# Routed expert blocks: hidden transposes and down products one block later, last additions split anew, one choice ahead of a copy

## The chip, the cores and the metric

One core of a Trainium2 chip runs the whole program in one launch. The metric is the device time of an execution in microseconds, median over the runs. TensorE (PE) multiplies matrices into PSUM, VectorE (DVE), ScalarE (ACT) and GpSimd (POOL) work on vectors, and SyncE (SP) issues most of the DMAs. Each engine works through its own list of instructions in order, and engines wait for each other on semaphores.

## The reference, cut to what matters

Eight sequences of 128 tokens with 128 features go through gated cross-attention with 16 heads and then through a mixture of experts:

```python
x = x + tanh(g_xattn[0]) * attention(layernorm(x), ctx, ctx, mask, Wq, Wk, Wv, Wo, 16)
h = layernorm(x)                                    # 1024 tokens x 128
shared = (silu(h @ shared_gate.T) * (h @ shared_up.T)) @ shared_down.T
probs = sigmoid(h @ router_w.T + routing_bias)      # 8 experts
scores, indices = top_k(probs, 2); scores = scores / sum(scores)
g = silu(einsum('th,ehi->tei', h, gate_w)); u = einsum('th,ehi->tei', h, up_w)
combined = einsum('tei,eih,te->th', g * u, down_w, w)   # w: scores at the two chosen experts
x = x + tanh(g_ffn[0]) * (shared + combined)
```

The hidden width of each expert is 256. All is in float32.

## The kernel before

**Attention and routing.** The attention runs over pairs of batches. As soon as a batch is through, its second layernorm, its logits, the choice of two experts for each token and the place of each token in its expert's list are worked out, in five groups: batches 0 and 1, 2 and 3, 4 and 5, then 6, then 7. `choose_steps(r)` (L1002) makes the choice of group r on VectorE in five steps, the last of which writes `hot`; `ranks(r)` (L451) counts on TensorE; `place(r)` (L1045) turns the ranks into slots; `scatter(r)` (L1356) on GpSimd writes the rows of the chosen tokens to the DRAM table `xs` with indirect DMAs. GpSimd's list after the attention is: scatters of group 2 (batches 4 and 5) with the two reciprocal deviations of batches 6 and 7 between them, the counts of groups 2 and 3, the scatters of batches 6 and 7 (L1431 to L1438). On VectorE the choice of group 2 stands around the copy `copy_pt(14, 2)` (L955, L1214 to L1220), which moves transposed probabilities from PSUM to SBUF for TensorE.

**Routed blocks.** The rows in `xs` are sorted by expert and cut into 23 blocks (`BLOCKS`) of 128 slots; how many of them hold rows depends on the data. `EARLY` is 5: so many blocks are fetched before batches 6 and 7 are placed. For each block n:

- SyncE fetches its rows from `xs` into buffer n modulo 8 of `xg` (`gather`, L290). From block 8 on it first waits until the result of block n-8 has been written, since that write reads its row numbers from the same buffer.
- TensorE transposes the rows (`block_transpose`, L631; "gather transpose"), ScalarE and VectorE split them into a high and a low part (L848, L1243), and TensorE makes gate and up products in three passes (`block_gate_up`, L640).
- ScalarE applies SiLU (L854), VectorE multiplies (`block_hidden`, L1248) to `hid`.
- TensorE transposes `hid` (`block_hidden_transpose`, L648; "hidden transposes", two, into the one bank `hT_bank`), VectorE copies the result to SBUF (`block_hidT`, L1254), and TensorE makes the down product (`block_down`, L657).
- ScalarE scales it by the token's weight into `y_sb` (`block_y`, L860), and GpSimd writes it with an indirect DMA to the DRAM table `ys` (L1441).

The order is written out by hand: iteration n of TensorE's loop (L673) issues the gather transpose of block n+2, gate and up of block n+1, the down product of block n-1 and the hidden transposes of block n. ScalarE and VectorE have loops of the same kind (L869, L1269). Products of the shared expert (`shared_pass`, `down_step`) are put in at iteration 3 and after the loop.

**The end.** When the last block with rows is written (SyncE's waits at L314), SyncE loads `ys` in four parts of two batches (`load_y`, L221). GpSimd adds the first chosen expert's rows to `x_sb` (L1447), then VectorE adds the second's (L1292), and for each half VectorE adds the shared expert's product from PSUM (`add_shared`, L1205). `store_out` (L225) stores two batches at a time, two on SyncE's queue and two on ScalarE's.

Of the kernel before, what the change touches and what calls it, by code (L numbers as in the profile page):

```python
# [6 lines left out]
ALU = mybir.AluOpType  # L7
# [28 lines left out]
LAST = len(ROUTED) - 1  # L36
SEEN = 6
EARLY = (SEEN * P * TOP_K - E_ROUTED * (P - 1)) // P + 1
PAD_ROWS = SLOTS // P // 5
IN_FLIGHT = 8  # L40
FEWEST = TOKENS * TOP_K // P // IN_FLIGHT
# [14 lines left out]
def build(nc, x, ctxT, mask, wqT, wkT, wvT, woT, gu, down, routerT, rows, ident, before, out):  # L56
    with ExitStack() as stack:
# [6 lines left out]
        def sem(name):  # L64
            return stack.enter_context(nc.semaphore(name))
# [19 lines left out]
        x_sb = sb("x_sb", [P, B, P])  # L85
# [124 lines left out]
        tx_done, xghi_ready, xglo_ready = sem("tx_done"), sem("xghi_ready"), sem("xglo_ready")  # L210
        bg_done, sil_ready, hid_ready = sem("bg_done"), sem("sil_ready"), sem("hid_ready")
        th_done, hidT_ready, yb_done, y_ready = sem("th_done"), sem("hidT_ready"), sem("yb_done"), sem("y_ready")
        first_added, second_added = sem("first_added"), sem("second_added")

        xs = nc.dram_tensor("xs", (SLOTS, WIDTH), F32).ap()
        ys = nc.dram_tensor("ys", (TOP_K * TOKENS, P), F32).ap()
# [7 lines left out]

        def store_out(engine, n):  # L225
            tiles = slice(2 * n, 2 * n + 2)
            engine.wait_ge(acc_done, 1 + n // 2)
            engine.dma_start(out[:, tiles, :], x_sb[:, tiles, :]).then_inc(out_sem, 16)

        block = stack.enter_context(nc.Block())  # L230
# [94 lines left out]
        def _(pe):  # L325
# [322 lines left out]
            def block_hidden_transpose(n):  # L648

                pe.wait_ge(hid_ready, n + 1)  # L650
                if n:
                    pe.wait_ge(hidT_ready, n)
                for c in range(2):
                    mm = pe.transpose(hT_bank[:, c * P:(c + 1) * P], hid[n % 2][:, c * P:(c + 1) * P], ident_sb[:])
                mm.then_inc(th_done, 1)
# [17 lines left out]
            for n in range(BLOCKS):  # L673
                if n + 2 == EARLY:
                    pe.wait_ge(h_done, 1)
                    shared_pass(1, 0)
                    shared_pass(1, 1)
                if n + 2 < BLOCKS:
                    block_transpose(n + 2)
                if n + 1 < BLOCKS:  # L680
                    block_gate_up(n + 1, experts[n + 1])
                if n + 2 < BLOCKS:
                    experts[n + 2] = block_expert(n + 2)
                if n:
                    block_down(n - 1, experts.pop(n - 1))
                block_hidden_transpose(n)
            pe.wait_ge(xglo_ready, BLOCKS)
            shared_pass(2, 0)
            block_down(BLOCKS - 1, experts[BLOCKS - 1])
            shared_pass(2, 1)  # L690
            pe.wait_ge(hid_ready, BLOCKS)
            shared_pass(3, 0)
            shared_pass(3, 1)
            down_step(0)
# [4 lines left out]
        def _(act):  # L699
# [169 lines left out]
            for n in range(BLOCKS):  # L869
                if n + 2 < BLOCKS:  # L870
                    block_hi(n + 2)
                if n + 1 < BLOCKS:
                    block_silu(n + 1)
                if n:
                    block_y(n - 1)
                if n == 0:
                    silu(0)
                if n + 2 == EARLY:
                    silu(1)
            block_y(BLOCKS - 1)  # L880
            for unit in range(2, 4):
                silu(unit)
# [5 lines left out]
        def _(dve):  # L888
# [215 lines left out]
            def run(steps, count):  # L1104
                for _ in range(count):
                    next(steps, None)

            def finish(steps):
                for _ in steps:
                    pass  # L1110
# [102 lines left out]
            mask_max(15, PAIRS - 1, 3, chain(after(2, x2_lo, 2), after(5, copy_o, 13, 1)))  # L1213
            recips(15, 3, (0,))  # L1214
            choice = choose_steps(2)
            run(choice, 1)
            copy_pt(14, 2)
            run(choice, 1)
            recips(15, 3, (1,))
            finish(choice)  # L1220
            finish(weight_steps(2))
            place(2)
            add_attention(B - 2, use)
# [43 lines left out]
            run(last_table, 3)  # L1267
            block_hidden(0)
            for n in range(BLOCKS):  # L1269
                if n:  # L1270
                    block_hidT(n - 1)
                run(last_table, 1)
                if n + 2 < BLOCKS:
                    block_lo(n + 2)
                if n == 1:
                    hidden(0)
                run(last_table, 1)
                if n + 1 < BLOCKS:
                    block_hidden(n + 1)
                run(last_table, 1)  # L1280
                if n + 1 == EARLY:
                    hidden(1)
                if n == 2 * EARLY:
                    quota_steps()
            block_hidT(BLOCKS - 1)
            for unit in range(2, 4):
                hidden(unit)
            for half in range(2):
                for n in (2 * half, 2 * half + 1):
                    tiles = slice(2 * n, 2 * n + 2)  # L1290
                    dve.wait_ge(first_added, n + 1)
                    dve.tensor_tensor(x_sb[:, tiles, :], y_of[:, tiles, 1, :], x_sb[:, tiles, :], ALU.add).then_inc(second_added, 1)  # L1292
                dve.wait_ge(second_added, 2 * half + 2)
                add_shared(half)


        @block.gpsimd
        def _(pool):
# [140 lines left out]
            for n in range(BLOCKS):  # L1439
# [1 line left out]
                pool.indirect_dma_start(out=ys, out_offset=bass.IndirectOffsetOnAxis(  # L1441
                    ap=xg[n % IN_FLIGHT][:, P:P + 1].bitcast(U32), axis=0), in_=y_sb[n % IN_FLIGHT][:], in_offset=None,
                    bounds_check=TOP_K * TOKENS - 1, oob_is_err=False).then_inc(y_out[n % IN_FLIGHT], 16)
            for n in range(4):
                tiles = slice(2 * n, 2 * n + 2)
                pool.wait_ge(in_y[n], 16)
                pool.tensor_tensor(x_sb[:, tiles, :], y_of[:, tiles, 0, :], x_sb[:, tiles, :], ALU.add).then_inc(first_added, 1)  # L1447


# [37 lines left out]
```

## Time and profile before

| what | value |
|---|---|
| median of 3 runs | 179.69 us (179.23 to 180.6) |
| the profiled execution | 180.42 us, its span 178.4 us |
| busy share of the span | PE 92%, DVE 71%, ACT 61%, POOL 62% |
| chain that ended last | PE 50%, DVE 13%, ACT 9%, DMA 9%, POOL 9%, issue 6% |
| granted TensorE clock | full until TensorE's work is over, half in the last slice |
| routed blocks | first gather transpose 123.74, last down product 165.36 |
| TensorE's last product ends | 171.7 us |

Times in the rows are microseconds from the start of the span. A busy TensorE is one with instructions in flight, not one at its peak. PE rows are matmuls (a transpose is one too), PEld rows their weight loads. The span is the time from the first to the last instruction of the profiled execution.

### The profile page before, as it was taken

How to read it: one execution, taken by the hardware profiler on the slowest of the kernel's cores; microseconds unless marked ns; L12 is line 12 of the kernel's file. 1: busy time of each engine (PE TensorE's matmuls, PEld its weight loads, DVE VectorE, ACT ScalarE, POOL GpSimd, SP SyncE). 2: the span in 40 equal slices, each digit the busy share in tenths (PEclk: the TensorE clock that was granted, in tenths of full speed). 3: DMA queues.
4: the chain of work that ended last, by engine and by line, in shares of the span. 5: the costliest groups of instructions: out<-in, count | busy, mean ns of one | idle time of the engine just before them, and what ended most of it. 6: DMA issues, size and time to landing. Idle time of an engine off the chain costs nothing.

```text
span 178.4 us, 4673 instructions
## 1 busy us (share of the span) xinstructions
PE 164.0 (92%) x1412; PEld 139.4 (78%) x1412; DVE 127.0 (71%) x611; ACT 109.3 (61%) x403; POOL 111.4 (62%) x141
## 2 busy tenths in 40 slices
PE   7899889999999999999999999988999999998950
PEld 7687669997879998879998778976586878786840
DVE  2789988755898776788676878877947666664344
ACT  4566997558697457787547878535446656564300
POOL 3665799846786825867714858686544665666460
PEclk9999999999999999999999999999999999999995
DMA  5899995810000000000000000013222322221253
GB/s 164 252 371 371 416 397 215 338 73 0 18 2 5 13 2 4 30 21 21 24 4 0 15 21 17 15 49 86 66 77 65 72 61 72 66 64 42 53 189 118
DMA packets 11095, 17.34 MB, mean 97 GB/s; under 512 B 2075, under 2 KB 6945, under 8 KB 10944
## 3 DMA queue, kind: packets, MB, share of 16 engines
q1 hardware_dynamic: 9504, 14.59, 24.3%
q0 software_dynamic: 1280, 2.20, 3.7%
q8 instruction: 12, 0.20, 0.5%
q10 hardware_dynamic: 288, 0.26, 0.4%
q14 instruction: 11, 0.09, 0.2%
HBM read 9.99 MB, written 7.51 MB: 98 GB/s over the span
## 4 chain that ended last, share of the span: by engine, by line
PE 50%; DVE 13%; ACT 9%; DMA 9%; POOL 9%; issue 6%; SPq 1%; POOLq 0%
PE misc L408 8%; PE s_even L371 6%; PE o_bank L397 6%; ACT probs L727 4%; PE pt L382 4%; DMA ys<-probsT,xg 3%; PE pt L663 3%; PE proj_q L328 3%; DMA wq_raw<-wqT 3%; PE proj_k L328 3%; DVE probs L939 3%; POOL ys L1441 2%; PE proj_k L330 2%; PE proj_k L329 2%; PE proj_q L330 2%
## 5 line engine op out<-in xcount | busy, mean ns | idle before, releaser
L727 ACT ACTIVATE probs<-probs,negmax 128x128 f32<-128x128 f32 x128 | 50.0, 395 | 8.5 <-DVE negmax L939 8.5
L1332 POOL TENSOR_TENSOR probs<-probs,rinv 128x512 f32<-128x512 f32 x32 | 33.1, 1046 | 24.6 <-DVE rinv L953 24.4
L1441 POOL DMA_INDIRECT ys<-probsT,xg x23 | 22.5, 979 | 17.3 <-issue 10.2
L727 ACT ACTIVATION_READ_ACCUMULATOR probs<-probs,negmax 128x1 f32 x128 | 24.5, 191 | 0.0
L939 DVE CUSTOM_DVE_ANT_0 probs<-s_even,mask 128x128 f32<-128x128 f32 x64 | 18.1, 283 | 3.8 <-issue 3.8
L1362 POOL DMA_INDIRECT xs<-xrow,slot x16 | 16.2, 1011 | 6.8 <-issue 3.9
L382 PE MATMUL pt<-ident_sb,probs 128*128 128x128 f32 x128 | 17.6, 277 | 1.6 <-POOL probs L1332 1.1
L371 PE MATMUL s_odd<-kT,qT 64*128 64x128 f32 x128 | 18.5, 285 | 0.0
L371 PE MATMUL s_even<-kT,qT 64*128 64x128 f32 x128 | 18.5, 285 | 0.0
L939 DVE CUSTOM_DVE_ANT_0 probs<-s_odd,mask 128x128 f32<-128x128 f32 x64 | 18.2, 284 | 0.0
L663 PEld LDWEIGHTS pt<-down_sb,v 128*128 128x128 f32 x92 | 12.1, 190 | 7.6 <-issue 7.5
L716 ACT COPY qT<-proj_q 128x512 f32<-128x512 f32 x12 | 7.1, 588 | 16.8 <-PE proj_q L330 16.8
L371 PEld LDWEIGHTS s_even<-kT,qT 64*128 64x128 f32 x128 | 15.4, 187 | 2.1 <-issue 1.4
L663 PE MATMUL pt<-down_sb,v 128*128 x92 | 15.7, 293 | 1.5 <-DVE v L1258 1.5
L382 PEld LDWEIGHTS pt<-ident_sb,probs 128*128 128x128 f32 x128 | 14.1, 141 | 3.4 <-issue 1.8
L397 PE MATMUL o_bank<-probsT,v 128*64 128x128 f32 x240 | 16.4, 279 | 0.0
L397 PEld LDWEIGHTS o_bank<-probsT,v 128*64 128x64 f32 x240 | 12.8, 136 | 3.4 <-issue 2.5
L371 PEld LDWEIGHTS s_odd<-kT,qT 64*128 64x128 f32 x128 | 15.4, 187 | 0.0
L408 PE MATMUL misc<-wo_sb,oT 128*128 128x128 f32 x112 | 14.3, 281 | 1.0 <-DVE oT L961 1.0
L408 PEld LDWEIGHTS misc<-wo_sb,oT 128*128 128x128 f32 x112 | 13.0, 192 | 2.0 <-DVE oT L961 1.7
L864 ACT ACTIVATE probsT<-pt,xg 128x128 f32<-128x128 f32 x23 | 8.5, 368 | 6.6 <-PE pt L663 4.9
L926 DVE COPY kT<-proj_k 128x512 f32<-128x512 f32 x12 | 8.3, 692 | 5.8 <-PE proj_k L330 5.6
(287 smaller groups left out, 457.2 us busy)
## 6 DMA issues: line engine op xcount, KB each, us to landing
xs<-pad SPq DMA_DIRECT2D x5, 858.0 KB, 5.6
xg<-xs SPq DMA_DIRECT2D x23, 66.0 KB, 1.9
down_sb<-down SPq DMA_DIRECT2D x1, 1152.0 KB, 9.0
probs<-ys SPq DMA_DIRECT2D x4, 256.0 KB, 4.1
gu_raw<-gu SPq DMA_DIRECT2D x3, 256.0 KB, 6.4
wk_raw<-wkT SPq DMA_DIRECT2D x2, 256.0 KB, 4.0
wq_raw<-wqT SPq DMA_DIRECT2D x2, 256.0 KB, 5.4
mask<-mask SPq DMA_DIRECT2D x8, 64.0 KB, 2.0
```

The costliest lines, as they stand in the source:

```text
L328: pe.matmul(dst, a_hi, b_hi, start=True, stop=False)
L371: mm = pe.matmul(s_bank[odd][:, j * P:(j + 1) * P], qT[rows, 4 * half + j, i * P:(i + 1) * P], kT[rows, 4 * half + j, i * P:(i + 1) * P], ...
L382: mm = pe.transpose(pt_bank[u][:, j * P:(j + 1) * P], probs[:, r, 4 * u + j, :], ident_sb[:])
L397: mm = pe.matmul(o_of.get(g, o_bank)[DK * odd:DK * (odd + 1), j * P:(j + 1) * P], v_sb[i][:, h * DK:(h + 1) * DK], probsT[:, half, 2 * j + ...
L408: mm = pe.matmul(misc[:, 0:P], oT[:, c // 4, c % 4, :], wo_sb[:, c, :], start=(c == 0), stop=(c == CHUNKS - 1))
L663: mm = pe.matmul(y_bank[:, 0:P], hidT[n % 2][:, c, :], down_sb[:, bass.ds(e * I_FFN + c * P, P)], start=(c == 0), stop=(c == 1))
L727: e = act.activation(probs[:, r, l, :], probs[:, r, l, :], ACT.Exp, bias=negmax[:, r, l:l + 1], scale=-1.0, accum_out=rowsum[:, r, l:l + 1])
L864: act.activation(y_sb[n % IN_FLIGHT][:], y_bank[:, 0:P], ACT.Copy, scale=xg[n % IN_FLIGHT][:, P + 1:P + 2]).then_inc(y_ready, 1)
L939: dve.tensor_tensor_reduce(probs[:, r, l, :], s_bank[l % 2][:, (l // 2) * P:(l // 2 + 1) * P], mask_sb[r // 2][:], -1.0, HUGE, ALU.add, AL ...
L1332: pool.tensor_tensor(quad, quad, rinv[:, r, 4 * u:4 * u + 4].unsqueeze(2).to_broadcast([P, 4, P]), ALU.mult).then_inc(norm_done, 1)
L1362: pool.indirect_dma_start(out=xs, out_offset=bass.IndirectOffsetOnAxis(ap=slot[:, b, k:k + 1], axis=0), in_=xrow[:, b, k, :], in_offset=No ...
L1441: pool.indirect_dma_start(out=ys, out_offset=bass.IndirectOffsetOnAxis(ap=xg[n % IN_FLIGHT][:, P:P + 1].bitcast(U32), axis=0), in_=y_sb[n ...
```

## The change

It has three parts. In the routed loop, from block 3 on (`FIRST` is 3), TensorE issues the hidden transposes of block n-1 in iteration n, right behind gate and up of block n+1, and then the down product of block n-2, where it had issued the down product of n-1 and the hidden transposes of n. ScalarE's and VectorE's lists follow. After the loop the last hidden transposes and the two last down products stand between the shared products. In the routing of batches 4 and 5 VectorE's copy `copy_pt(14, 2)` goes from the second step of the choice to behind it. At the end VectorE adds both experts' rows for the first four batches after the shared part; for the last four GpSimd adds the two experts' rows to each other and VectorE adds the sum. A store now waits for the additions of its own two batches.

```diff
...
 LAST = len(ROUTED) - 1
 SEEN = 6
 EARLY = (SEEN * P * TOP_K - E_ROUTED * (P - 1)) // P + 1
+FIRST = EARLY - 2
 PAD_ROWS = SLOTS // P // 5
 IN_FLIGHT = 8
 FEWEST = TOKENS * TOP_K // P // IN_FLIGHT
...
-        first_added, second_added = sem("first_added"), sem("second_added")
+        rows_added, pair_added = sem("rows_added"), sem("pair_added")
 
         xs = nc.dram_tensor("xs", (SLOTS, WIDTH), F32).ap()
         ys = nc.dram_tensor("ys", (TOP_K * TOKENS, P), F32).ap()
...
 
         def store_out(engine, n):
             tiles = slice(2 * n, 2 * n + 2)
-            engine.wait_ge(acc_done, 1 + n // 2)
+            engine.wait_ge(rows_added, (2, 4, 5, 6)[n])
             engine.dma_start(out[:, tiles, :], x_sb[:, tiles, :]).then_inc(out_sem, 16)
 
         block = stack.enter_context(nc.Block())
...
                     block_gate_up(n + 1, experts[n + 1])
                 if n + 2 < BLOCKS:
                     experts[n + 2] = block_expert(n + 2)
-                if n:
+                if n > FIRST:
+                    block_hidden_transpose(n - 1)
+                if 1 <= n <= FIRST:
                     block_down(n - 1, experts.pop(n - 1))
-                block_hidden_transpose(n)
+                if n < FIRST:
+                    block_hidden_transpose(n)
+                if n > FIRST + 1:
+                    block_down(n - 2, experts.pop(n - 2))
             pe.wait_ge(xglo_ready, BLOCKS)
             shared_pass(2, 0)
-            block_down(BLOCKS - 1, experts[BLOCKS - 1])
+            block_hidden_transpose(BLOCKS - 1)
+            block_down(BLOCKS - 2, experts.pop(BLOCKS - 2))
             shared_pass(2, 1)
-            pe.wait_ge(hid_ready, BLOCKS)
+            block_down(BLOCKS - 1, experts.pop(BLOCKS - 1))
             shared_pass(3, 0)
             shared_pass(3, 1)
             down_step(0)
...
                     block_hi(n + 2)
                 if n + 1 < BLOCKS:
                     block_silu(n + 1)
-                if n:
+                if 1 <= n <= FIRST:
                     block_y(n - 1)
+                if n > FIRST + 1:
+                    block_y(n - 2)
                 if n == 0:
                     silu(0)
                 if n + 2 == EARLY:
                     silu(1)
+            block_y(BLOCKS - 2)
             block_y(BLOCKS - 1)
             for unit in range(2, 4):
                 silu(unit)
...
             mask_max(15, PAIRS - 1, 3, chain(after(2, x2_lo, 2), after(5, copy_o, 13, 1)))
             recips(15, 3, (0,))
             choice = choose_steps(2)
-            run(choice, 1)
-            copy_pt(14, 2)
-            run(choice, 1)
+            run(choice, 2)
             recips(15, 3, (1,))
             finish(choice)
+            copy_pt(14, 2)
             finish(weight_steps(2))
             place(2)
             add_attention(B - 2, use)
...
             run(last_table, 3)
             block_hidden(0)
             for n in range(BLOCKS):
-                if n:
+                if 1 <= n <= FIRST:
                     block_hidT(n - 1)
                 run(last_table, 1)
                 if n + 2 < BLOCKS:
...
                 if n == 1:
                     hidden(0)
                 run(last_table, 1)
+                if n > FIRST:
+                    block_hidT(n - 1)
                 if n + 1 < BLOCKS:
                     block_hidden(n + 1)
                 run(last_table, 1)
...
             block_hidT(BLOCKS - 1)
             for unit in range(2, 4):
                 hidden(unit)
-            for half in range(2):
-                for n in (2 * half, 2 * half + 1):
-                    tiles = slice(2 * n, 2 * n + 2)
-                    dve.wait_ge(first_added, n + 1)
-                    dve.tensor_tensor(x_sb[:, tiles, :], y_of[:, tiles, 1, :], x_sb[:, tiles, :], ALU.add).then_inc(second_added, 1)
-                dve.wait_ge(second_added, 2 * half + 2)
-                add_shared(half)
+            def add_rows(n, k):
+                tiles = slice(2 * n, 2 * n + 2)
+                dve.wait_ge(in_y[n], 16)
+                dve.tensor_tensor(x_sb[:, tiles, :], y_of[:, tiles, k, :], x_sb[:, tiles, :], ALU.add).then_inc(rows_added, 1)
+
+            add_shared(0)
+            for n in range(2):
+                dve.wait_ge(acc_done, 1)
+                add_rows(n, 0)
+                dve.wait_ge(rows_added, 2 * n + 1)
+                add_rows(n, 1)
+            add_shared(1)
+            dve.wait_ge(acc_done, 2)
+            for n in range(2, 4):
+                dve.wait_ge(pair_added, n - 1)
+                add_rows(n, 0)
 
 
         @block.gpsimd
...
                 pool.indirect_dma_start(out=ys, out_offset=bass.IndirectOffsetOnAxis(
                     ap=xg[n % IN_FLIGHT][:, P:P + 1].bitcast(U32), axis=0), in_=y_sb[n % IN_FLIGHT][:], in_offset=None,
                     bounds_check=TOP_K * TOKENS - 1, oob_is_err=False).then_inc(y_out[n % IN_FLIGHT], 16)
-            for n in range(4):
+            for n in range(2, 4):
                 tiles = slice(2 * n, 2 * n + 2)
                 pool.wait_ge(in_y[n], 16)
-                pool.tensor_tensor(x_sb[:, tiles, :], y_of[:, tiles, 0, :], x_sb[:, tiles, :], ALU.add).then_inc(first_added, 1)
+                pool.tensor_tensor(y_of[:, tiles, 0, :], y_of[:, tiles, 0, :], y_of[:, tiles, 1, :], ALU.add).then_inc(pair_added, 1)
 
 
 def kernel(x, ctx_1024, fside_Bx1xSxS2_0, g_xattn, g_ffn, L0_xattn_Wq, L0_xattn_Wk, L0_xattn_Wv, L0_xattn_Wo,
```

## Rows read from the trace of the kernel before

**Rows 1.** Timeline, 148 to 152, one loop iteration: start, duration, engine, line, operation, operands.
```profile
148.71 0.27 PE L638 MATMUL misc<-ident_sb,xg 128*128 128x128 f32 x1
...
149.53 0.69 PE L663 MATMUL pt<-down_sb,v 128*128 x4
...
150.06 0.38 PE L654 MATMUL pt<-ident_sb,kT 128*128 128x128 f32 x2
...
150.26 0.37 ACT L864 ACTIVATE probsT<-pt,xg 128x128 f32<-128x128 f32 x1 [0.15 <-PE pt L663]
...
150.48 0.42 DVE L1258 COPY v<-pt 128x256 f32<-128x256 f32 x1
...
151.09 0.66 PE L663 MATMUL pt<-down_sb,v 128*128 x4
...
151.40 0.98 POOL L1441 DMA_INDIRECT ys<-probsT,xg  x1 [0.58 <-issue]
```

**Rows 2.** The chain of waits, 148 to 154: start, duration, what.
```profile
148.31 3.27 DMA ys<-probsT,xg
...
151.74 1.82 DMA xg<-xs
...
153.61 0.33 PE o_bank L638
```

**Rows 3.** One line, L1441 (block writes), 140 to 160.
```profile
DMA to landing us min/median/max: 2.2/2.3/3.3
```

**Rows 4.** One line, L293 (block fetches), 138 to 158: who waited (us, times), and landing.
```profile
  PEld o_bank L638: 0.3, 1
...
DMA to landing us min/median/max: 1.8/2.0/2.7
```

**Rows 5.** Timeline, TensorE, a down product that waits.
```profile
136.70 0.71 PE L663 MATMUL pt<-down_sb,v 128*128 x4 [0.34 <-DVE v L1258]
```

**Rows 6.** Timeline: low part of block 6; gather transposes of blocks 10 and 22.
```profile
134.81 0.29 DVE L1245 TENSOR_TENSOR xg_lo<-o_bank,xg_hi 128x128 fp32r<-128x128 f32 x1 [0.31 <-ACT xg_hi L852]
...
140.55 0.27 PE L638 MATMUL o_bank<-ident_sb,xg 128*128 128x128 f32 x1
...
159.98 0.27 PE L638 MATMUL o_bank<-ident_sb,xg 128*128 128x128 f32 x1
```

**Rows 7.** The chain of waits, 164 to 171.
```profile
164.19 2.76 DMA ys<-probsT,xg
...
167.23 3.70 DMA probs<-ys
```

**Rows 8.** Timeline, block 20's down product, and the last additions.
```profile
162.30 0.71 PE L663 MATMUL pt<-down_sb,v 128*128 x4
...
171.00 3.13 POOL L1447 TENSOR_TENSOR x_sb<-probs,x_sb 128x256 f32<-128x256 f32 x4 [2.78 <-DMA probs<-ys]
171.76 1.79 DVE L1292 TENSOR_TENSOR x_sb<-probs,x_sb 128x256 f32<-128x256 f32 x2 [2.26 <-POOL x_sb L1447]
...
174.26 0.75 DVE L1292 TENSOR_TENSOR x_sb<-probs,x_sb 128x256 f32<-128x256 f32 x2
...
175.04 0.75 DVE L1209 SCALAR_TENSOR_TENSOR x_sb<-proj_q,tanh_g,x_sb 128x512 f32<-128x512 f32 x1
```

**Rows 9.** Timeline, 111 to 115, the choice for batches 4 and 5.
```profile
111.42 2.10 POOL L1332 TENSOR_TENSOR probs<-probs,rinv 128x512 f32<-128x512 f32 x2
111.52 0.69 DVE L957 COPY probsT<-pt 128x512 f32<-128x512 f32 x1
...
113.08 0.49 DVE L1026 TENSOR_TENSOR hot<-rows_sb,chosen_at 128x32 bf16<-128x32 f32 x1
...
113.67 0.17 PE L463 MATMUL proj_q<-hotsum,ones_bf 128*128 128x8 bf16 x1
...
114.88 1.01 POOL L1362 DMA_INDIRECT xs<-xrow,slot  x1 [1.36 <-DVE slot L1053]
```

**Rows 10.** The chain of waits, GpSimd's count of batch 6.
```profile
121.44 0.21 POOL hotsum L1354
```

## The prediction

> **What bounds it now.** I read the busy times by engine first, then the chain of waits, then the timeline of the routed blocks. TensorE is busy for 92% of the span (the table above), so the loop over 23 blocks looks like TensorE's. One iteration shows how: gather transpose at 148.71, down product at 149.53, hidden transposes at 150.06, the next down product at 151.09 [rows 1]: 1.56 us an iteration, 1.53 in the neighbouring one, mean 1.545. Inside it the hidden transposes at 150.06 feed a VectorE copy at 150.48 to 150.90, and the down product at 151.09 uses that copy: the gather transpose and the gate-up product fill just this gap. So the loop has two nearly equal limits, and this is the one the change relaxes.
>
> A third limit is outside the engines. Block n's result lets block n+8's rows be fetched, because both use one of eight buffers. The chain shows that turn once: the indirect write of block 10 starts at 148.31 and takes 3.27, the fetch of block 18 starts at 151.74 and takes 1.82, and TensorE begins block 18's transpose at 153.61, having waited [rows 2]. The median write takes 2.3 and the median fetch 2.0 [rows 3, 4]; only that one gather transpose of the whole stretch had to wait [rows 4]. What matters is how much room the other turns had.
>
> **The turn, worked out.** From the end of ScalarE's copy of y (150.26+0.37 = 150.63) to the start of GpSimd's write (151.40) is 0.77 [rows 1]. The chain has 0.16 from the landing of the write to the fetch (151.58 to 151.74) and 0.05 from the fetch's landing to the transpose [rows 2]. With medians: 0.77+2.3+0.16+1.95+0.05 = 5.2 us. The down product starts 0.82 into its iteration (149.53-148.71) and y is finished 1.10 after it (150.63-149.53) [rows 1].
>
> Before: block n's down product runs in iteration n+1, block n+8's gather transpose opens iteration n+6. The turn needs 0.82+1.10+5.2 = 7.1 us and has five iterations, 7.7: 0.6 to spare at the median, nothing with a 3.27 write, as seen.
>
> After: from block 3 on the down product runs in iteration n+2, behind hidden transposes of 0.22, thus at 1.04. The turn needs 1.04+1.10+5.2 = 7.35 and has four iterations, 6.2. **It does not fit.** Each turn waits 1.15 us, and the loop's pace becomes 7.35/4 = 1.84 us an iteration wherever such turns follow on each other.
>
> **Parts of the change.** (a) *The loop up to the last fetch.* Removed: waits of TensorE on VectorE's hidden copy, of which the one ahead of the down product at 136.70 is shown (0.34 idle, 0.5 with the drained pipeline) [rows 5]; there are two more, 0.28 near 146.4 and 0.60 near 163.8. Ahead of the first stands a limit that stays: block 6's low part, at 134.81 for 0.29 [rows 6], comes behind a wide SiLU on ScalarE, and block 6's gate-up cannot precede 135.15. Then come 0.71 of it, 0.22 transposes, 0.5 down product, which puts block 8's gather transpose at 136.6 to 136.75, and two iterations later block 10's at about 139.85, 0.7 earlier than its 140.55 [rows 6]. From there the turns are 10 to 14 to 18 to 22 in gather transposes four blocks apart, three turns: 139.85+3x7.35 = 161.9, against 159.98 now [rows 6]: +1.95. The other ladders (11, 15, 19) give within 0.3 of it. (b) *The order at the end.* SyncE's last wait is for the write of block 20, at 164.19 for 2.76, and then the loads of y, 3.70 to the first [rows 7]: the blocks after 20 don't set the end. Block 20's down product is now at 162.30 [rows 8], 2.32 after block 22's gather transpose. In the new order come 0.11 gather, 0.71 gate-up 21, 0.22, 0.50, 0.71 gate-up 22, 0.22 transposes of block 20 at +2.25; the transposes of block 21 follow one down product later, but share one PSUM bank and wait for the copy, 1.03 behind as in [rows 1] (150.06 to 151.09): +3.28; then 0.22, and the down product at +3.50. That is +1.2. Sum of (a) and (b) +3.15; one long write such as the 3.27 that already cost a wait will lie on a turn in most executions, for which I add 0.15: **+3.3**. Bounds: all transfers at their minima (2.2 and 1.8) give +2.1; writes and fetches as long as in this execution block by block, its 3.27 write and 2.7 fetch among them, give +4.0.
>
> The later order on ScalarE and VectorE costs nothing by itself: the y copy stands behind the same SiLU, the hidden copy ahead of the hidden product delays that by 0.3, and its reader is the gate-up product two iterations on. If that cover went, at most 0.3 per block would show. GpSimd's 23 writes are the same and come less often than now. SyncE issues the same 23 fetches in order; each now waits behind its later write, which is the turn above.
>
> (c) *The choice ahead of the copy.* The 0.69 copy at 111.52 goes behind the choice. The choice's last operation, hot, starts at 113.08 and takes 0.49 for 32 elements a partition; GpSimd's normalising, two instructions in 2.10 from 111.42, ends just then, at 113.52 [rows 9]. VectorE must wait for the exponentials until 112.13 anyway, so hot starts only 0.1 earlier, and I take it to end no sooner. And the ranks on TensorE start at 113.67, right behind four transposes: TensorE's own order holds them. So the gain is 0 (bound: -0.1). The copy then lies between hot and the weights and slots: GpSimd's scatter at 114.88, which had waited 1.36 for the slots [rows 9], comes 0.64 later. From it GpSimd runs through to the count of batch 6 at 121.44 [rows 10], in the chain of waits all the way, and TensorE's ranks and the first fetch behind it are late next. **+0.6**; bounds 0 (a cover I did not see) and +0.7.
>
> The Trainium skill, "SBUF — State Buffer", section "Who interferes with whom", says that a VectorE instruction with two SBUF inputs and a GpSimd instruction that reads SBUF block each other wholly, whoever issues first. The row of hot agrees. Without that rule hot would keep its 0.49 and end 0.1 sooner, and (c) would be 0.1 less.
>
> (d) *The last additions.* Now, after the first load lands at 170.93: four GpSimd additions from 171.00, 3.13 together; two VectorE additions beside them, 1.79 together; a shared part of 0.75; two additions undisturbed, 0.75 together; and the last shared part at 175.04, 0.75 [rows 8], so the last store goes at 4.86 behind the load. New: the first shared part is done before. The loads land at most 0.8 apart (GpSimd's four additions follow on each other). VectorE: four additions of 0.38 with 0.05 between, to +1.7; shared part to +2.5; GpSimd adds pairs from +1.6 and +2.4 to +3.2; VectorE's fifth addition, disturbed, 0.9, to +3.4; the sixth to +3.8. 4.86-3.8 = **-1.1**. Bounds: -1.4 undisturbed, -0.5 if every VectorE addition costs 0.9. The second shared part needs TensorE's last product. That ends 9.4 after block 20's down product now (171.7, the table) and no more than that in the new order: 165.6+0.6+9.4 = 175.6 at the latest, wanted at 174.8+1.7 = 176.5: covered by 0.9. The first one's products end 1.9 sooner, 173.7, and its 0.75 fits ahead of the load at 174.8.
>
> By the same rule of "SBUF — State Buffer", the pair additions and VectorE's would exclude each other: the fifth then ends at about +3.5 and the sixth at +3.9, 0.1 more than the sum has.
>
> **Sum.** 3.3+0.6-1.1 = +2.8 us on this execution's 180.42 (span 178.4 and 2.0 around it): 183.2. The median of the runs is 179.69, 0.73 lower, so **182.5**.
>
> **Rivals.** *1. The turn is hidden (not slower).* Place: the gather transposes of blocks 11 to 22. If the transit were under 4.05 instead of 5.2, the turn would fit four iterations; then the removed waits (about 0.9) nearly pay for (b), +0.3 in all, and with (d) and (c) the change gives -0.8 to -0.2, 179.2 at the middle. For it: before, all but one turn were covered. Against: the minima already sum to 0.77+2.2+0.16+1.8 = 4.9 [rows 1 to 4]. But rows of one execution could mislead me on which write frees which fetch, and TensorE's order could be looser. 0.20; of this 0.08, with (c) at 0 and (d) at -1.4, gives more than 1% faster. *2. Only the choice is free:* TensorE or the loads hide it; 182.5-0.6 = 181.9. For it: nothing in the chain; chance 0.12. *3. Turns as long as the worst seen:* +4.0, with (d) at -0.5: +4.1, 183.8. For it the 3.27 write; against it that more waiting means fewer transfers at once. 0.16. *4. The change in the tail fails* because the second shared part waits for TensorE: TensorE's work would have to stretch by 0.9. 0.02, near 183.5.
>
> **Numbers.** My forecast has 0.50 (181.5 to 183.4), the rivals 0.20, 0.12, 0.16, 0.02. About 1% (1.8 us) is what a measurement here can tell from none: bounds 177.9 and 181.5. Slower by more: 0.44 of the forecast, 0.08 of rival 2, rivals 3 and 4 whole: 0.70. Within: the other 0.06 and 0.04, and 0.12 of rival 1: 0.22. Faster: 0.08. The range leaves out the faster part of rival 1 and the far end of rival 3: 179.3 to 184.1. Where the turn decides (0.80) its own range is 180.9 to 184.1.
>
> **What would show it.** Waits of TensorE's weight load for the fetch, ahead of the gather transposes of blocks 11, 15, 17 to 19 and 21, together 2.5 to 4.5 us, where there was one of 0.3. No waits ahead of down products in the loop, save the last two blocks. The scatter behind the slots near 115.5 and the first fetch 0.6 later. From the first load of y to the last store 3.8. I am wrong if the gather transposes come 1.55 apart throughout, or if ranks for batches 4 and 5 start before 113.5.

## The result, and the profile after

| | before | after |
|---|---|---|
| median of 4 runs each | 180.11 us (179.23 to 180.6) | 184.42 us (184.35 to 185.16) |
| ratio | | 1.0241 [1.0201, 1.028] |
| the profiled execution, its span | 180.42, 178.4 | 185.16, 183.2 |

The change makes the kernel 4.3 us slower. The forecast was slower by 2.8, with 182.5 and a range that ends at 184.1: the direction and the mechanism hold, the size does not.

The two spans differ by 4.8. Cut at events that both traces have, that is:

| stretch | before | after | difference | forecast |
|---|---|---|---|---|
| start to the exponentials of batches 4 and 5 | 110.81 | 111.52 | +0.7 | none |
| from there to the first gather transpose | 12.93 | 13.58 | +0.65 | +0.6 |
| from there to block 20's write landed | 43.21 | 47.64 | +4.4 | +3.3 |
| to the first load of y landed | 3.98 | 3.82 | -0.2 | none |
| to VectorE's last addition | 4.86 | 3.65 | -1.2 | -1.1 |
| to the end of the span | 2.59 | 2.97 | +0.4 | none |

The exponentials are ScalarE's for the logits of batches 4 and 5, 110.81 and 111.52. The first line is no part of the change: it arises in the first 12 us, when weights are loaded (ScalarE's first copy of weights starts at 3.98 before and at 4.61 after). Without it the stretches add up to 4.1, where the medians differ by 4.3.

**The turn.** The line of the gather transposes after, with what its engines waited for (the columns are us, times; TensorE's matmuls and its weight loads are counted apart, so 12 is six blocks):

```profile
  DMA xg<-xs: 9.5, 12
```

Before, one block waited 0.3 [rows 4]. Now six do, blocks 11, 15, 17, 18, 21 and 22, and the weight load alone waits 5.3 of the 9.5. The chain of waits after (start, us, what) has three times a write, a fetch and the gather transpose that waits for it:

```profile
139.41 2.31 DMA ys<-probsT,xg
...
141.88 1.91 DMA xg<-xs
143.84 0.33 PE misc L639
144.17 0.37 PE s_even L329
...
146.85 0.77 POOL ys L1461
...
148.33 0.76 POOL ys L1461
...
149.80 0.78 POOL ys L1461
...
151.29 3.71 DMA ys<-probsT,xg
...
155.16 2.00 DMA xg<-xs
157.21 0.33 PE o_bank L639
...
160.21 2.37 DMA ys<-probsT,xg
...
162.74 2.10 DMA xg<-xs
164.89 0.33 PE o_bank L639
```

Block 3's write brings block 11, block 10's brings block 18, and block 14's brings block 22. Between them the chain runs along GpSimd's writes of blocks 7 to 10, which start 1.48 apart, the pace of TensorE's iterations there; block 10's starts 0.77 behind ScalarE's copy of y as well, as the prediction has it. 143.84 is block 11 and the transpose of block 15 comes at 151.20, 7.36 later, the turn worked out in the prediction as 7.35. The transpose of block 14 is at 148.46, though, and that of block 18 at 157.21, 8.75 later, because the write of block 10 takes 3.71, where [rows 2] had 3.27. Block 22 comes another 7.68 later. Of the chain from 139.4 to the landing of block 20's write, half is now writes and fetches (16.5 of 33.3 us); over the whole span the page has DMA at 13% of the chain, where it had 9%, and TensorE at 46%, where it had 50%:

```profile
PE 46%; DMA 13%; DVE 11%; ACT 10%; POOL 8%; issue 8%; SPq 1%; DVEq 0%; POOLq 0%; ACTq 0%
```

**The order at the end.** Block 20's down product, in the timeline of TensorE:

```profile
164.89 0.33 PE L639 MATMUL o_bank<-ident_sb,xg 128*128 128x128 f32 x1 [0.65 <-DMA xg<-xs]
...
168.24 0.41 PE L655 MATMUL pt<-ident_sb,kT 128*128 128x128 f32 x2 [0.16 <-DVE v L1267]
168.73 0.37 PE L664 MATMUL pt<-down_sb,v 128*128 x1
```

That is 3.84 behind block 22's gather transpose, where it was 2.32 [rows 6, 8]: +1.5, with +1.2 forecast.

**The choice**, in the timeline (start, duration, engine, line, operation):

```profile
112.12 2.04 POOL L1352 TENSOR_TENSOR probs<-probs,rinv 128x512 f32<-128x512 f32 x2
...
113.61 0.60 DVE L1036 TENSOR_TENSOR hot<-rows_sb,chosen_at 128x32 bf16<-128x32 f32 x1
...
114.13 0.68 DVE L967 COPY probsT<-pt 128x512 f32<-128x512 f32 x1
114.31 0.17 PE L464 MATMUL proj_q<-hotsum,ones_bf 128*128 128x8 bf16 x1
...
116.12 1.00 POOL L1382 DMA_INDIRECT xs<-xrow,slot  x1 [1.96 <-DVE slot L1063]
```

Against [rows 9]: `hot` now takes 0.60 in place of 0.49 and ends at 114.21, just where GpSimd's normalising ends (114.16). That is 2.69 behind the exponentials, where it was 2.76, so it gains 0.1 at most; the ranks stay behind it; and GpSimd waits 1.96 for the slots in place of 1.36. Here the Trainium skill, "SBUF — State Buffer", section "Who interferes with whom", agrees with the trace: an instruction of VectorE with two SBUF inputs is blocked by one of GpSimd that reads SBUF, until that one is through.

**The last additions**, timeline:

```profile
175.37 0.75 DVE L1219 SCALAR_TENSOR_TENSOR x_sb<-proj_k,tanh_g,x_sb 128x512 f32<-128x512 f32 x1 [0.47 <-PE proj_k L583]
176.65 1.68 DVE L1302 TENSOR_TENSOR x_sb<-probs,x_sb 128x256 f32<-128x256 f32 x4 [0.54 <-DMA probs<-ys]
177.94 1.65 POOL L1467 TENSOR_TENSOR probs<-probs 128x256 f32<-128x256 f32 x2 [3.63 <-DMA probs<-ys]
178.25 0.74 DVE L1219 SCALAR_TENSOR_TENSOR x_sb<-proj_q,tanh_g,x_sb 128x512 f32<-128x512 f32 x1
179.03 1.19 DVE L1302 TENSOR_TENSOR x_sb<-probs,x_sb 128x256 f32<-128x256 f32 x2
```

The first shared part lies ahead of the load, and the rest is over 3.65 behind it, as forecast (3.8), for 4.86 in [rows 8]. But then the span goes on for 2.97 instead of 2.59. The rows of GpSimd's and SyncE's closing drains (duration in ns, start) tell why. Before:

```profile
L57 POOLq DRAIN  x1: 4518/4518/4518, 173.0 to 173.0; - x1
...
L57 SPq DRAIN  x1: 7/7/7, 178.2 to 178.2; - x1
```

After:

```profile
L58 POOLq DRAIN  x1: 4377/4377/4377, 178.6 to 178.6; - x1
...
L58 SPq DRAIN  x1: 7/7/7, 182.2 to 182.2; - x1
...
L58 SPq EVENT_SEMAPHORE  x1: 17/17/17, 183.1 to 183.1; - x1
```

Before, GpSimd's drain is over at 177.5 and the last store, at 178.2, sets the end. After, the last store is in at 182.2, and the program waits for GpSimd until 183.0. Its last addition had ended at 179.59, 3.4 earlier. So GpSimd ends 0.8 behind the stores: from VectorE's last addition to the last store it takes 2.0 (180.22 to 182.2), less than the 2.4 of before, but the span takes 2.97.

### The profile page after: what moved, and what is told of

It reads as the page before. It is cut to its first block, busy times and chain, and to the rows that moved or that the text cites. A ratio compares the mean times of both kernels' runs of the same rounds, so it can differ in the third digit from the quotient of the medians.

```text
span 183.2 us, 4677 instructions
## 1 busy us (share of the span) xinstructions
PE 165.7 (90%) x1412; PEld 141.8 (77%) x1412; DVE 126.8 (69%) x613; ACT 108.6 (59%) x403; POOL 110.2 (60%) x139
## 4 chain that ended last, share of the span: by engine, by line
PE 46%; DMA 13%; DVE 11%; ACT 10%; POOL 8%; issue 8%; SPq 1%; DVEq 0%; POOLq 0%; ACTq 0%
PE misc L409 7%; ACT probs L734 6%; DMA ys<-probsT,xg 6%; PE s_even L372 6%; PE o_bank L398 5%; PE proj_q L329 4%; DMA xg<-xs 3%; PE proj_k L329 3%; PE pt L383 3%; DVE probs L949 3%; PE proj_q L330 3%; PE proj_q L331 3%; PE proj_k L331 3%; PE proj_k L330 3%; DMA probs<-ys 2%
## 5 line engine op out<-in xcount | busy, mean ns | idle before, releaser
L664 PE MATMUL pt<-down_sb,v 128*128 x92 | 14.4, 279 | 0.3 <-DVE v L1267 0.2
L1267 DVE COPY v<-pt 128x256 f32<-128x256 f32 x23 | 9.7, 423 | 6.4 <-PE pt L655 6.4
```

Of the source, the lines that this page charges most:

```text
L664: mm = pe.matmul(y_bank[:, 0:P], hidT[n % 2][:, c, :], down_sb[:, bass.ds(e * I_FFN + c * P, P)], start=(c == 0), stop=(c == 1))
```

## The experiments

Each group of kernels ran on one chip, with runs of the kernel before among them. What the kernel before takes differs from group to group (180.0, 180.2, 182.3, 184.0, 184.6), so ratios are compared, not times; a difference in us below is the ratio's, times the time before there.

| kernel | us | before there | ratio |
|---|---|---|---|
| loop part alone | 185.75 | 182.28 | 1.0184 [1.0138, 1.0231] |
| choice alone | 182.99 | 182.28 | 1.0031 [0.9999, 1.0064] |
| last additions alone | 181.43 | 182.28 | 0.9949 [0.9911, 0.9988] |
| changed, 12 buffers | 183.36 | 182.28 | 1.003 [0.9987, 1.0073] |
| changed, again | 184.21 | 180.00 | 1.0222 [1.0178, 1.0266] |
| changed, new order from block 15 | 180.09 | 180.00 | 1.0012 [0.9984, 1.004] |
| before, 12 buffers | 179.18 | 180.00 | 0.9962 [0.9933, 0.9991] |
| before, additions, 12 buffers | 178.70 | 180.00 | 0.9928 [0.9903, 0.9953] |

**The parts one by one.** The first three kernels are the kernel before with the hunks of one part of the diff, shown ahead, and no others: those with `FIRST` and `block_y`, `block_hidT`; the one around `copy_pt(14, 2)`; those with `add_rows`, `pair_added` and `store_out`.

```diff
+FIRST = EARLY - 2
...
+                if n > FIRST:
+                    block_hidden_transpose(n - 1)
```

> The kernel before with the loop part of the change alone. Theory (the turn through write and fetch has four iterations instead of five and does not fit): it carries nearly all of the loss, in the profile +4.4 us from the first gather transpose to the landing of block 20's write, so 184.2 to 184.9, with five or six waits of TensorE for fetches, 4 to 5 us together. Rival (the parts add up otherwise: the choice behind everything makes the fetches late): under +2 us.

Measured: +3.4 us (+4.4 were expected in the profile), and the gather transposes wait for fetches, as the source view of that line has it, 6.3 us over matmuls and weight loads (4 to 5 were expected):

```profile
  DMA xg<-xs: 6.3, 9
  issue: 1.3, 2
```

So the loop part alone makes the change slow, and by this wait.

```diff
-            run(choice, 1)
-            copy_pt(14, 2)
-            run(choice, 1)
+            run(choice, 2)
...
+            copy_pt(14, 2)
```

> The kernel before with the choice of batches 4 and 5 ahead of the copy alone. Theory: hot ends no sooner, the copy stands ahead of weights and slots, the scatter after the slots comes 0.5 to 0.7 later and so does the end: +0.6 us. Rival (the copy is hidden): within 0.2 us of before.

Measured: +0.57 us, the interval just touching none; in the trace the exponentials are followed by the first gather transpose 13.61 later, +0.68 on the 12.93 of before. Its `hot` takes 0.60 and GpSimd waits 1.96 for the slots, the same two numbers as in the whole change.

```diff
+            add_shared(0)
+            for n in range(2):
+                dve.wait_ge(acc_done, 1)
+                add_rows(n, 0)
+                dve.wait_ge(rows_added, 2 * n + 1)
+                add_rows(n, 1)
+            add_shared(1)
```

> The kernel before with the new split of the last additions alone. Theory: 3.7 us from the first load's landing to the last addition instead of 4.9: -1.1 us. Rival (the second shared part waits for TensorE's last product, or GpSimd and VectorE hold each other up): -0.5 to 0.

Measured: -0.93 us. From the load to the last addition 3.65, from there to the end 2.97: the same two numbers as in the whole change again, so the 0.4 at the end belongs to this part. Together the three parts give 1.84+0.31-0.51 = 1.6%, against 2.2 and 2.4% for the whole in its two comparisons. The three intervals together are 0.7% wide to each side, so the sum may be the whole; whether about 1 us comes only when the parts stand together stays open.

**Is it the buffers?** The ring gets four more, so that block n frees block n+12 and a turn has eight iterations.

```diff
-IN_FLIGHT = 8
+IN_FLIGHT = 12
...
+        xg += [xn_flat[:, i * WIDTH:(i + 1) * WIDTH] for i in range(IN_FLIGHT - KNOWN)]
```

> The changed kernel with 12 buffers in flight instead of 8, the four new ones in memory that the attention no longer needs, so a fetch waits for the write 12 blocks back. Theory (the turn): TensorE's waits for fetches in the loop go, the first gather transpose to the landing of block 20's write takes what it took before plus 0.3 to 1.2, the kernel comes to 180.0 to 181.0. Rival (the later order itself costs TensorE and VectorE time in each iteration): over 183.

Measured: of the 2.4% 0.3 stay, and no gather transpose waits for a fetch. The rest of the expectation missed. In us the kernel takes 183.36, on the rival's side of 183, though on a chip where the kernel before takes 182.28; and in its trace block 20's write starts 44.3 behind the first gather transpose (125.12 to 169.45), where it was 40.5 and at most 1.2 more was expected. That part is taken up below, under the pauses. The same on the kernel before, and with the additions:

> The kernel before with 12 buffers in flight instead of 8. Theory (in the kernel before the turn of 7.1 us had five iterations and fitted but for one write): the one wait for a fetch goes, -0.3 us. Rival (the turn did not matter there at all, or the earlier fetches disturb the writes): 0 or slower.

> The kernel before with the new split of the last additions and 12 buffers, no loop change and no change of the choice: the version that the theory gives as the fastest, -1.1 for the additions and -0.3 for the wait: 1.4 us under before, 5 to 6 under the changed kernel. Rival: only the additions count, -1.1.

Measured: -0.7 and -1.3 us (-0.3 and -1.4 were expected). Even before, the one wait of [rows 4] was worth 0.44 us of loop (43.21 to 42.77).

**Is it the turn's length?** The new order only from block 15 on. Blocks 15 and later free blocks 23 and later, which don't exist, so no turn is longer, while the order at the end is the changed one.

```diff
-FIRST = EARLY - 2
+FIRST = 15
```

> The changed kernel with FIRST = 15: the down products are one block later only from block 15 on, behind which no fetch depends on a write any more. Theory (the turn): no more waits for fetches than before (one, 0.3), the loop takes 0.6 to 1.0 more than before because of the order at its end, the kernel lies 2.5 to 3.5 us under the changed one, within 1 us of before. Rival (the later order costs time in itself): half of the blocks are late, so half of the loop's loss stays, about 1.5 to 2 us under the changed one.

> The changed kernel once more, beside the variants of it on the same chip. Theory and rival alike: 2.0 to 2.8% over before, waits for fetches in the loop of 4 to 6 us by TensorE's and its weight load's rows together.

Measured: the repeat of the changed kernel on this chip gives +4.0 us, this one +0.2. The line of the gather transposes, with nothing else altered in them:

```profile
  DMA xg<-xs: 0.8, 2
```

One block waits, block 18, as before the change (the rival's 1.5 to 2 us under the changed kernel did not come: it is 3.8). The loop takes 43.84, 0.6 more than before. That is the clearest of the results: the same instructions in the same late order cost 4 us where they lie on a turn and next to nothing where they don't.

**Why is the write of block 10 long?** In the traces of before and after a transfer of instructions, 16 KB on a queue of its own, lies beside it. The DMA queues (packets, MB, share of 16 engines) before, from 148.3 to 151.6:

```profile
q8 instruction: 1, 0.02, 1.8%
```

After, from 151.3 to 155.0:

```profile
q8 instruction: 1, 0.02, 1.6%
```

The fetch of block 17, in the same stretch, takes 3.0. In the 2.1 us after it there is no such transfer, and the fetch of block 18 takes 2.0. The packets show what holds the write up. Its queue, q0, after the change: from 152.7 to 153.1, from 153.1 to 153.85 (no line of q0), and from 153.88 to 154.0, when the transfer of q8, which starts at 152.99 and takes 0.93, is just over:

```profile
q0 software_dynamic: 30, 0.01, 14.6%
```

```profile
q0 software_dynamic: 2, 0.00, 2.4%
```

Thirty of the write's 32 packets are through by 153.05, and the last two come at 153.91, right behind that transfer. That is 0.9 of the 1.4 that this write takes too long; why it lands only 1.1 behind them is not shown. Its rows are not the reason, since with 0.01 MB it is smaller than a full block's 0.07. Block 10's write is long, 3.1 to 3.8, in all nine traces that show its landing, of both kernels and of the one before with 12 buffers. In the repeat of the changed kernel block 9's is longer still, 4.4, and the transfer, from 151.5 to 153.0, lies beside both.

To move that transfer, 36 tiny matmuls replace a warm-up near the end of the routing of the kernel before.

```diff
-            stay_warm(5)
+            for _ in range(36):
+                pe.matmul(s_bank[0][:, 0:E_ROUTED], ones_bf[:], ones_bf[:, 0:E_ROUTED], start=True, stop=True)
```

> The kernel before with 36 tiny matmuls in place of the five that keep TensorE warm ahead of the routed blocks: 52 instructions more on TensorE's list, under 1 us of time. In every trace so far a 16 KB transfer of the instruction queue q8 runs beside the write of block 10 and the fetch of block 17, and these take 0.9 and 0.7 longer than their neighbours. Theory (q8 carries TensorE's instructions, some 28 an iteration, and slows the small transfers beside it): the transfer comes about two iterations earlier, and with it the long write goes to block 8 and the long fetch to block 15. Rival (block 10's write is long for its rows or its place in GpSimd's list): it stays with block 10.

Measured, in one execution: the transfer and the long write both went to block 8. GpSimd's timeline and the queues from 150.1 to 152.9:

```profile
150.07 0.98 POOL L1442 DMA_INDIRECT ys<-probsT,xg  x1 [1.60 <-ACT probsT L865]
```

```profile
q8 instruction: 1, 0.02, 2.5%
```

This write takes 2.88, that of block 10 only 2.22, and the fetch of block 17, 2.7 before [rows 4], takes 1.39; the packets of block 15's fetch are spread over 1.0 (151.17 to 152.21) in place of 0.5, as expected. (The trace has only a part of the landing events of block 8's write, so 2.88 is the least that it took.) So the long transfers go with the transfer of instructions and not with the block, and more instructions on TensorE move it. That execution has pauses of its own (next), and it took 186.19 where the kernel before takes 184.03, more than the 1 us that was expected. The other traces bear it out: in all 16 of them this transfer starts while TensorE is between the gather transposes of blocks 14 and 17, here behind that of block 13 (150.30 to 150.56).

**Pauses that hid it.** Where the kernel before takes 184 us, the changed kernel with 12 buffers missed its expectation again, and so the kernel before was run there once more, with a profile, beside the former.

> The changed kernel with 12 buffers once more, for a profile free of the disturbance of the first one. Theory: no wait of TensorE for a fetch; from the first gather transpose to the landing of block 20's write 43.5 to 44.5 us (before 43.2, changed 47.6); 0 to 0.5% over before. Rival: over 45 us.

> The kernel before itself, for a profile on the same chip as the next one. The chips used so far take 180.0, 182.3 and 184.0 us for it. If the extra waits seen in the profiles of the slower chips (a copy that starts 1 us after the matmuls it waits for) belong to the chip, they stand in this trace too, if the chip is a slow one, and the loop to block 20's write takes over 43.8; on a fast chip it takes 43.2.

> The changed kernel with 12 buffers beside that profile. Theory: no wait for a fetch, and the loop to block 20's write within 1.5 us of the kernel before's on this chip. Rival (with 12 buffers something else in the late order costs as much as the fetches did): 3 us over it or more.

Measured: changed with 12 buffers 1.0037 [1.0004, 1.007] and 1.0021 [0.9993, 1.0049]; before against itself 0.9985 [0.993, 1.004]. The ratios are as expected. From the first gather transpose to block 20's write these took 46.53 (43.5 to 44.5 were expected: a miss), 47.65, and 46.24 in the unchanged kernel (over 43.8 was expected), which had taken 43.21, with no gather transpose waiting for its fetch in any of them. Beside each other the two kernels differ by 1.4, within the 1.5 expected. The timeline of the unchanged kernel in these runs:

```profile
144.11 0.69 PE L663 MATMUL pt<-down_sb,v 128*128 x4
...
144.64 0.38 PE L654 MATMUL pt<-ident_sb,kT 128*128 128x128 f32 x2
...
145.84 0.37 ACT L864 ACTIVATE probsT<-pt,xg 128x128 f32<-128x128 f32 x1 [1.15 <-PE pt L663]
145.89 0.42 DVE L1258 COPY v<-pt 128x256 f32<-128x256 f32 x1 [0.74 <-PE pt L654]
```

ScalarE's copy starts 1.04 after the product's last instruction, where [rows 1] has 0.04 (149.53+0.69 to 150.26). Such pauses are not the change's, since the unchanged kernel has them too. Whether they belong to a chip stays open, as does what they are: the groups of 184.0 and 184.6 us and the one of 180.2 us, below, bear the same chip number in the record.

**Where the 0.4 at the end goes.** The additions the other way round: both shared parts first, then GpSimd adds the pairs of the first four batches, so that it is through sooner, and VectorE the rest.

```diff
+            add_shared(0)
+            add_shared(1)
+            for n in range(2):
+                dve.wait_ge(pair_added, n + 1)
+                add_rows(n, 0)
+            for n in range(2, 4):
+                add_rows(n, 0)
+                add_rows(n, 1)
...
-            for n in range(2, 4):
+            for n in range(2):
```

> The kernel before with the additions split the other way round: both shared parts first, GpSimd adds the pairs of the first four batches, whose loads land first, VectorE those of the last four. Theory (the span ends 3.40 after GpSimd's last addition or 2.59 after VectorE's, whichever is later): GpSimd's end no longer counts, 2.4 to 2.6 from VectorE's last addition to the end, and from the first load's landing to it 3.3 to 3.5: the end 1.6 to 2.0 us after the landing sooner than in the kernel before, 0.5 to 0.9 better than the split of the change. Rival (the stores make the difference): still 2.97.

> The same with 12 buffers in flight: the version that should beat both kernels and all others, 1.0 to 1.4% under before. Rival: 12 buffers add nothing on top, 0.8 to 1.0%.

> The kernel before with the change's split of the additions and 12 buffers, on the same chip: 0.7% under before as on the other chip, 0.5 us or more over the run with the other split.

| kernel | us (before there: 180.17) | ratio | load to last addition | to the end |
|---|---|---|---|---|
| additions the other way | 179.26 | 0.9947 [0.9925, 0.9969] | 3.85 | 2.21 |
| the same, 12 buffers | 178.70 | 0.9911 [0.9877, 0.9945] | | |
| the change's additions, 12 buffers | 178.85 | 0.9929 [0.9903, 0.9956] | 3.65 | 2.97 |

The drain's part is as the theory has it, with 2.21 even less than the 2.4 to 2.6 expected: GpSimd's drain is over at 175.8, and SyncE's stores, at 176.8, set the end, in the rows of the closing instructions:

```profile
L57 POOLq DRAIN  x1: 4137/4137/4137, 171.7 to 171.7; - x1
...
L57 SPq DRAIN  x1: 7/7/7, 176.8 to 176.8; - x1
```

The additions' part missed, 3.85 where 3.3 to 3.5 were expected. The timeline has why:

```profile
171.03 1.40 POOL L1455 TENSOR_TENSOR probs<-probs 128x256 f32<-128x256 f32 x2 [2.87 <-DMA probs<-ys]
171.67 0.75 DVE L1209 SCALAR_TENSOR_TENSOR x_sb<-proj_q,tanh_g,x_sb 128x512 f32<-128x512 f32 x1 [1.04 <-PE proj_q L582]
172.46 2.35 DVE L1291 TENSOR_TENSOR x_sb<-probs,x_sb 128x256 f32<-128x256 f32 x6
```

VectorE's second shared part now stands ahead of its additions, and it waits for TensorE's last product until 171.67, 0.7 behind the load (170.95). It is over at 172.42, and only then, at 172.46, can the six additions begin. In sum it is 6.06 from the load to the end against 6.62 with the change's split and 7.45 before: 1.4 less than before (1.6 to 2.0 were expected), 0.56 less than the change's. In the time the two splits can't be told apart (0.9911 and 0.9929, intervals over each other; 0.15 us, where 0.5 or more were expected), and 0.9% is less than the 1.0 to 1.4% expected of the best, but both with 12 buffers beat before and after. The best measured version is the kernel before with this end and 12 buffers, 0.9% faster than before.

## Why the prediction was right in its sign and wrong in its size

- **The turn does not fit four iterations: right.** Waits at blocks 11, 15, 17, 18, 21 and 22 (11, 15, 17 to 19 and 21 were named), 5.3 us of waits by the weight load (2.5 to 4.5), a turn of 7.36 where no write is long (7.35; so close by luck, since it holds a refill of 0.2, below, against a fetch of 1.85 and a shorter copy), and both ways of taking the turn away, more buffers or the late order only where it frees nobody, take the loss away (0.3% and 0.1% left of 2.2 to 2.4%). Rival 1, a hidden turn, is out.
- **The waits on VectorE's hidden copy that go: right.** From the first gather transpose to block 10's it took 16.82 and takes 15.93, -0.9 (-0.7).
- **The size of (a): the step that failed.** From block 10's gather transpose to block 22's it took 19.42 and takes 23.86; 22.05 were forecast, three turns of 7.35. They are 7.43, 8.75 and 7.68. The step priced the transfers at medians, 2.3 and 1.95 (the median fetch of [rows 4] is 2.0), and a long write, 3.27-2.3 = 1.0 by its own rows, at 0.15, though it says that one will lie on a turn in most executions. But it is no matter of chance: the write of block 10 is long each time, because the instructions' transfer comes there, and block 10 lies on the ladder 10, 14, 18, 22, so its whole excess, 3.71-2.3 = 1.4, is paid in the second turn. The third turn's 0.33 is in part the refill: a gather transpose that waited starts with TensorE empty, and the down product comes 1.22 behind it, where it comes 1.04 behind one that didn't wait:

```profile
148.46 0.27 PE L639 MATMUL o_bank<-ident_sb,xg 128*128 128x128 f32 x1
...
149.50 0.61 PE L664 MATMUL pt<-down_sb,v 128*128 x4
...
157.21 0.33 PE L639 MATMUL o_bank<-ident_sb,xg 128*128 128x128 f32 x1 [0.16 <-DMA xg<-xs]
...
158.43 0.61 PE L664 MATMUL pt<-down_sb,v 128*128 x4
```

  The sum left these 0.2 out. The fetch of block 22, 2.10 for 1.95, is another 0.15. In all (a) came to +3.55 for +2.1, and (a) and (b) to +5.1 up to block 20's down product. Of this +4.4 stay, since the write of block 20 got shorter, 2.13 for the 2.76 of [rows 7]. That is luck, since no term of the sum has it. Before the change the next transfer of instructions starts at 164.84, beside the write of block 20 (164.19 to 166.95), and after it at 169.84, beside the write of block 19, which takes 2.6. The upper bound, +4.0, was worked out block by block from such rows and had the write of block 10 on the path, but with 3.27 in place of 3.71, shorter fetches and no refill. Rival 3, which has its price, was the nearest case, and had 0.16.
- **(b), the order at the end:** +1.5 for +1.2. The difference is refills: behind block 22's transpose, and behind block 21's hidden transposes, which had waited for VectorE's copy; block 20's down product starts 0.49 after those (168.24 to 168.73), where 0.22 was counted.
- **(c), the choice:** +0.65 for +0.6, alone +0.57. In the traces of both `hot` ends at most 0.1 sooner and the slots come later, so rival 2 is out.
- **(d), the last additions:** -1.2 for -1.1 in what the step covered. It ended at the last addition, though, and behind that GpSimd's drain gave 0.4 back.
- **Rival 4** didn't come: the second shared part starts as soon as VectorE's four additions are done (178.25).
- **Rival 1's share of 0.08** for more than 1% faster had no ground in its own terms: with (c) at 0 and (d) at -1.4 it comes to -1.1 us, 0.6%.

The terms that were off are +1.1 in the loop and +0.4 at the end; with +0.05 in (c), -0.2 in the load of y and -0.1 in (d) they make the forecast's 2.8 the 4.1 between the two traces. The medians differ by 4.3.

By the Trainium skill, "DMA: Bandwidth & Descriptors", section "Anatomy of one DMA — SWDGE (gpsimd) path", a DMA issued by GpSimd takes about 2.0 us and its bytes over 436 KB per us, which makes an estimate of 2.15 for a write of 64 KB. The median write, 2.3, agrees within 0.15; the writes on which this result hangs, at 3.3 to 3.7, don't.

## What to carry to other kernels

When work is moved later in a loop, draw the ring of buffers first: what the moved step frees, and in how many iterations that is wanted; a slack at the median of 0.6 us was used up by one more iteration. Price the transfers on such a ring block by block from the trace, since a long one that recurs at the same block lies on the path each time, and add the refill of the engine that waited (0.2 here). Follow the last step of a change to the end of the span: what drains or lands behind it can take the gain.

## What the hardware showed that was not expected

- A transfer of TensorE's instructions lengthens a small write beside it by 0.6 to 1.4 us (2.88, 3.27, 3.71 against a median of 2.3): two of its 32 packets come only when that transfer is over. It moves with the count of instructions, so that it comes at the same block each time.
- GpSimd is done 3.4 us after its last addition in three traces (174.13 to 177.5, 179.59 to 183.0, 172.43 to 175.8). With its additions earlier, that time lies under the stores.
- The same kernel takes 180.0 to 184.6 us in different groups of runs, and in an execution of 184.2 ScalarE starts 1.04 behind TensorE's product at one place, where 0.04 is usual. Whether that is the chip is not shown.
